# Expert weights in four buffers, and their loads queued block by block

## The chip, the cores and the metric

The kernel runs on one NeuronCore of a Trainium2 chip. The metric is the device time of one execution in microseconds; the program runs on one core, so its time is that core's. Three runs of the kernel before took 1793.85, 1797.31 and 1800.29 us, with a median of 1797.31.

## The reference

A small language-model tower of two layers works on 16 sequences of 128 tokens with rows of 192 numbers, in float32: embedding and layer norm, a Mamba block with a gated feed-forward, a mixture of experts, causal attention with 12 heads, and a second mixture of experts beside a shared gated feed-forward. The change is in the two mixtures. Both send each token to its two best experts:

```python
# layer 0: 8 experts, inner width 768;  x: the normed rows, e: an expert
y_e = relu(x @ W1[e].T + b1[e]) @ W2[e].T + b2[e]
# layer 1: 16 experts, inner width 512
y_e = (silu(x @ w1[e].T) * (x @ w3[e].T)) @ w2[e].T
# both: e, f are the router's two best of the token, g and k its weights
h = h + g * y_e + k * y_f
```

## The kernel before

Tokens are held as rows, 128 to a tile, 16 tiles. For each mixture the router gives every token a place in a DRAM array `sorted`, where each expert has a region of its own; GpSimd scatters the normed rows there (line 381). The array is then worked through in blocks of 128 rows, each of one expert: 40 blocks in the first mixture (`NB0`), 48 in the second (`NB1`). `rid` and `eid` hold the first row and the expert of each block. The results are stored in `expert`, a DRAM array of blocks, and gathered and added at the end.

All engines run the loop over blocks in pairs; block 0 of a pair uses the buffers with k = 0, the other those with k = 1. For one pair:

- SyncE (`expert_loads`, lines 301 to 327) loads the rows of both blocks (`xb`, 96 KB each, line 316), reads both expert numbers into registers, loads both first weights (`ew_in`, line 321: 576 KB in the first mixture, 768 KB in the second, over 96 partitions), then both second weights (`ew_out`, line 326: 675 KB with the biases in the first mixture, 384 KB in the second, over 128 partitions). Before each load it waits until its buffer is free. All of these go to one queue in program order.
- TensorE (`expert_blocks`) multiplies the turned rows with the first weight (24 matmul instructions a block in the first mixture, 32 in the second, line 715), turns the rows of the next pair (`turn`, line 978), and then makes the output products with the second weight (12 and 8 instructions a block).
- ScalarE applies Relu with the bias, which is part of `ew_out` (line 657, six instructions a block), or Silu in the second mixture (line 701). It waits for the second weight first in the first mixture.
- VectorE (`expert_rows_out`) copies the turned rows out of PSUM (line 1518), multiplies the two halves in the second mixture (line 1526), and adds the output bias (line 1537) or copies the output (line 1535) into `yb`, of which there are two. Before that it waits until `yb` was stored. Its drain then releases the second weight's buffer (semaphore `s_w2f`, line 1539). TensorE's drain (line 993) releases the first weight's (`s_w1f`).
- GpSimd (`store_blocks`) stores `yb` (line 468), waits for the landing and releases `yb`, one block after the other.

The buffers have two of each kind. The semaphores `s_w1`, `s_w2`, `s_w1f` and `s_w2f` exist once for each mixture and each k.

Of the kernel before, what the change touches and what calls it, by code (L numbers as in the profile page):

```python
# [9 lines left out]
ALU = mybir.AluOpType  # L10
AXX = mybir.AxisListType.X
ds = bass.ds

P = 128
B = 16
D = 192
# [41 lines left out]
def tower(nc, tok, seg, tok_tab, seg_tab, pos_tab, consts, rows, cols, w_pick, w_in, w_gate, w_x, w_dt, w_out,  # L58
          w_up, w_gf, w_down, w_r1, w_r2, w_qk, w_v, w_proj, w_g, w_s1, w_s3, w_s2, e0_in, e0_out, e1_in, e1_out,
          out):  # L60
    with ExitStack() as ctx:
# [42 lines left out]
        ew_in = [w[0:KH, :] for w in ew_in_all]  # L104
# [17 lines left out]
        def part(n, words, parts=P):  # L122
            return arena[0:parts, n:n + words]
# [28 lines left out]

        xb = [part(6144 + 256 * k, D) for k in range(2)]
# [47 lines left out]
        s_w1 = [[sem(f"s_w1_{m}{k}") for k in range(2)] for m in range(2)]  # L201
        s_w2 = [[sem(f"s_w2_{m}{k}") for k in range(2)] for m in range(2)]
        s_xb = [[sem(f"s_xb_{m}{k}") for k in range(2)] for m in range(2)]
        s_w1f = [[sem(f"s_w1f_{m}{k}") for k in range(2)] for m in range(2)]
        s_w2f = [[sem(f"s_w2f_{m}{k}") for k in range(2)] for m in range(2)]
# [80 lines left out]
        def _(sp):  # L286
# [205 lines left out]
        def _(act):  # L492
# [159 lines left out]
            with act.Fori(0, NB0 // 2) as i:  # L652
                for k in range(2):
                    act.wait_ge(s_w2[0][k], i * 16 + 16)
                    act.wait_ge(s_bh[0], i * 2 + k + 1)
                    for f in range(EF0):
                        act.activation(hbT[k][:, f, :], ps[:, 1 + 2 * k + f // 4, (f % 4) * P:(f % 4 + 1) * P], ACT.Relu,  # L657
                                       bias=ew_out[k][:, EF0 * D + f:EF0 * D + f + 1])
                    act.drain().then_inc(s_ba[0], 1)
# [46 lines left out]
        def _(pe):  # L706
# [259 lines left out]
            def expert_blocks(m, nb, fg, gated):  # L966
                for k in range(2):
                    pe.sem_inc(s_xbf[m][k], 1)
                    pe.sem_inc(s_w1f[m][k], 1)
                    pe.sem_inc(s_w2f[m][k], 1)  # L970
                n_in = fg * P

                def turn(i):

                    for k in range(2):
                        pe.wait_ge(s_xb[m][k], i * 16 + 16)
# [4 lines left out]
                def pair(i, more):  # L981
                    for k in range(2):
                        pe.wait_ge(s_bx[m], i * 2 + k + 1)
                        pe.wait_ge(s_w1[m][k], i * 16 + 16)
                        for half in range(2 if gated else 1):
                            for f in range(fg):
                                bank = 1 + 2 * k + (half if gated else f // 4)
                                base = 2 * n_in * half
                                last = accumulate(ps[:, bank, (f % 4) * P:(f % 4 + 1) * P],
                                                  [(ew_in[k][:, base + c * n_in + f * P:base + c * n_in + (f + 1) * P], xbT[k][:, c, :])  # L990
                                                   for c in range(2)])
                        last.then_inc(s_bh[m], 1)
                        pe.drain().then_inc(s_w1f[m][k], 1)
                    if more:
                        turn(i + 1)
# [151 lines left out]
        def _(ve):  # L1147
# [363 lines left out]
            def expert_rows_out(m, nb, gated):  # L1511
# [3 lines left out]
                def turn(i):  # L1515
                    for k in range(2):
                        ve.wait_ge(s_bt[m], i * 2 + k + 1)
# [4 lines left out]
                def pair(i, more):  # L1522
                    if gated:
                        for k in range(2):
                            ve.wait_ge(s_bg, i * 2 + k + 1)
# [3 lines left out]
                    if more:  # L1529
                        turn(i + 1)  # L1530
                    for k in range(2):
                        ve.wait_ge(s_by[m], i * 2 + k + 1)
                        ve.wait_ge(s_ybf[m][k], i + 1)
                        if gated:
                            last = ve.tensor_copy(yb[k], ps[:, 5 + k, 0:D])  # L1535
                        else:
                            last = ve.tensor_tensor(yb[k], ps[:, 5 + k, 0:D], ew_out[k][:, EF0 * D + EF0:], ALU.add)
                        last.then_inc(s_yb[m], 1)
                        ve.drain().then_inc(s_w2f[m][k], 1)

                turn(0)
                with ve.Fori(0, nb // 2 - 1) as i:
                    pair(i, True)
                pair(nb // 2 - 1, False)
# [212 lines left out]
```

## Time and profile before

| | |
|---|---|
| median of three runs | 1797.31 us |
| the profiled execution | 1797.96 us, its span 1796.3 us |
| mean granted TensorE clock | 0.847 of full speed |
| TensorE matmul busy | 1335.5 us (74%) |
| VectorE / ScalarE / GpSimd busy | 819.6 / 496.1 / 495.2 us |
| DMA, mean over the span | 85 GB/s, 152.92 MB |
| first expert stage | from 698 to 972 us |
| second expert stage | from 1441 to 1742 us |

The profile is of one execution. Busy time is what an engine spends in instructions that compute; times in the rows are microseconds from the start of the span. An idle stretch is put down to what ended it: `<-DMA ew_in<-in_e_in` is the landing of that transfer, `<-issue` nothing that the profile shows. `POOL` is GpSimd, `DVE` VectorE, `ACT` ScalarE, `PE` TensorE, `PEld` its weight loads and `SPq` SyncE's sequencer, which issues the loads.

### The profile page before, as it was taken

How to read it: one execution, taken by the hardware profiler on the slowest of the kernel's cores; microseconds unless marked ns; L12 is line 12 of the kernel's file. 1: busy time of each engine (PE TensorE's matmuls, PEld its weight loads, DVE VectorE, ACT ScalarE, POOL GpSimd, SP SyncE). 2: the span in 40 equal slices, each digit the busy share in tenths (PEclk: the TensorE clock that was granted, in tenths of full speed). 3: DMA queues.
4: the chain of work that ended last, by engine and by line, in shares of the span. 5: the costliest groups of instructions: out<-in, count | busy, mean ns of one | idle time of the engine just before them, and what ended most of it. 6: DMA issues, size and time to landing. Idle time of an engine off the chain costs nothing.

```text
span 1796.3 us, 23568 instructions
## 1 busy us (share of the span) xinstructions
PE 1335.5 (74%) x7336; PEld 911.8 (51%) x7336; DVE 819.6 (46%) x1551; ACT 496.1 (28%) x834; POOL 495.2 (28%) x394
## 2 busy tenths in 40 slices
PE   0656787777778673877884678989988878999960
PEld 0211232332333263877774464756657468888850
DVE  2488975865888752111111735355453312222212
ACT  0435455446435201222221213315150100101000
POOL 4655743544544441000002400000001500000025
PEclk9868787888889785999997668897988889999985
DMA  5200000000000016777774100000000267888853
GB/s 117 40 1 1 0 1 0 1 1 1 1 1 1 12 43 191 236 211 224 229 226 131 50 0 1 1 0 0 0 1 12 97 167 219 240 233 241 239 145 94
DMA packets 56059, 152.92 MB, mean 85 GB/s; under 512 B 9632, under 2 KB 30880, under 8 KB 51200
## 3 DMA queue, kind: packets, MB, share of 16 engines
q1 hardware_dynamic: 44096, 127.80, 25.1%
q0 software_dynamic: 11904, 24.40, 4.7%
q8 instruction: 30, 0.49, 0.1%
q14 instruction: 29, 0.24, 0.0%
HBM read 133.09 MB, written 19.07 MB: 85 GB/s over the span
## 4 chain that ended last, share of the span: by engine, by line
PE 34%; DMA 23%; DVE 15%; issue 11%; POOL 5%; ACT 3%; POOLq 3%; DVEq 3%; SPq 1%; ACTq 1%; PEldq 0%
PE ps L715 23%; DMA expert<-arena 21%; DVE arena L1417 4%; PE ps L843 3%; PE ps L1075 2%; POOL arena L480 2%; DVE ps L1412 2%; PE ps L868 1%; DMA ew_in<-in_e_in 1%; ACT arena L583 1%; PE ps L1067 1%; DVE st L1173 1%; POOL h_rows L346 1%; ACT arena L677 1%; PE ps L710 1%
## 5 line engine op out<-in xcount | busy, mean ns | idle before, releaser
L715 PE MATMUL ps<-arena,ew_in 96*128 96x128 f32 x2496 | 308.5, 283 | 41.3 <-DMA ew_in<-in_e_in 25.0
L715 PEld LDWEIGHTS ps<-arena,ew_in 96*128 96x128 f32 x2496 | 294.4, 196 | 58.5 <-DMA ew_in<-in_e_in 34.0
L1417 DVE TENSOR_TENSOR_SCAN arena<-arena,ps 128x1024 f32<-128x1024 f32 x96 | 219.5, 2287 | 13.4
L715 PE MATMUL ps<-xTF,wreg 96*128 96x512 f32 x352 | 204.0, 726 | 9.5 <-DVE arena L1573 4.6
L843 PE MATMUL ps<-arena,pick 32*128 32x512 f32 x384 | 133.9, 781 | 94.9 <-DVE arena L1417 91.9
L468 POOL DMA_DIRECT2D expert<-arena x88 | 47.9, 544 | 543.1 <-DVE arena L1535 190.7
L381 POOL DMA_INDIRECT sorted<-x_rows,row_i x64 | 63.5, 992 | 416.8 <-DVEq L1322 398.1
L583 ACT ACTIVATE arena<-ps,wreg 128x508 f32<-128x508 f32 x192 | 121.0, 681 | 203.9 <-PE ps L855 203.1
L715 PE MATMUL ps<-xT,wreg 96*128 96x512 f32 (+3 forms) x296 | 134.8, 602 | 29.1 <-ACT arena L544 15.6
L715 PE MATMUL ps<-ew_out,arena 128*128 128x192 f32 x864 | 152.7, 333 | 1.0 <-issue 0.5
L715 PEld LDWEIGHTS ps<-ew_out,arena 128*128 128x128 f32 x864 | 144.1, 195 | 1.6 <-issue 0.8
L855 PE MATMUL ps<-arena,pick 32*128 32x512 f32 x384 | 135.4, 785 | 8.1 <-POOLq L389 7.3
L715 PEld LDWEIGHTS ps<-xTF,wreg 96*128 96x128 f32 x352 | 75.4, 228 | 107.8 <-issue 90.1
L843 PEld LDWEIGHTS ps<-arena,pick 32*128 32x128 f32 x384 | 35.9, 221 | 173.9 <-issue 166.5
L657 ACT ACTIVATE arena<-ps,ew_out 128x128 f32<-128x128 f32 x240 | 66.4, 376 | 206.2 <-DMA ew_out<-in_e_out 158.0
L1412 DVE TENSOR_TENSOR ps<-ps,arena 128x1024 f32<-128x1024 f32 x96 | 117.1, 1220 | 9.5 <-PE ps L843 4.1
L1526 DVE TENSOR_TENSOR arena<-arena,ps 128x512 f32<-128x512 f32 x48 | 33.0, 688 | 180.0 <-ACTq L702 179.5
L715 PEld LDWEIGHTS ps<-xT,wreg 96*128 96x128 f32 (+1 forms) x296 | 58.6, 209 | 102.9 <-issue 59.9
L701 ACT ACTIVATE arena<-ps 128x512 f32<-128x512 f32 x48 | 28.7, 598 | 279.7 <-PE ps L715 279.7
L408 POOL TENSOR_TENSOR ew_out<-arena 128x1024 f32<-128x1024 f32 x32 | 75.9, 2372 | 99.8 <-DVE arena L1417 98.1
L1518 DVE COPY arena<-ps 96x256 f32<-96x256 f32 x88 | 37.0, 421 | 143.3 <-PE ps L978 130.8
L408 POOL TENSOR_TENSOR ew_in<-arena 128x1024 f32<-128x1024 f32 x32 | 76.6, 2394 | 90.1 <-DVE arena L1417 89.3
(199 smaller groups left out, 1699.6 us busy)
## 6 DMA issues: line engine op xcount, KB each, us to landing
ew_in<-in_e_in SPq DMA_DIRECT2D x48, 768.0 KB, 6.1
ew_out<-in_e_out SPq DMA_DIRECT2D x40, 675.0 KB, 4.3
ew_in<-in_e_in SPq DMA_DIRECT2D x40, 576.0 KB, 5.6
ew_out<-in_e_out SPq DMA_DIRECT2D x48, 384.0 KB, 4.0
arena<-sorted SPq DMA_DIRECT2D x88, 96.0 KB, 2.6
expert<-arena POOLq DMA_DIRECT2D x88, 96.0 KB, 4.2
sorted<-zero SPq DMA_DIRECT2D x26, 96.0 KB
wreg<-in_w_s SPq DMA_DIRECT2D x3, 768.0 KB, 11.3
```

The lines of the kernel that those rows point to most:

```text
L381: pool.indirect_dma_start(sorted_rows[m], bass.IndirectOffsetOnAxis(row_i[:, r, t:t + 1], 0), x_rows[:, t, :], None).then_inc(s_scat[m], 16)
L408: pool.tensor_tensor(hc[k % 6].rearrange("p (x t) -> p x t", x=2), hid[k % 3].rearrange("p (x t) -> p x t", x=2), Ct[c % 2].rearrange("p ( ...
L468: pool.dma_start(expert_rows[m][ds((i * 2 + k) * P, P), :], yb[k]).then_inc(s_yo[m][k], 16)
L480: pool.indirect_dma_start(g[:, t, :], None, expert_rows[m], bass.IndirectOffsetOnAxis(pos_i[:, r, t:t + 1], 0)).then_inc(s_g[m], 16)
L583: act.activation(o[:, :, 1:P], t[:, :, 1:P], ACT.Exp, scale=neg_a[:, j:j + 1]).then_inc(s_dec, 1)
L657: act.activation(hbT[k][:, f, :], ps[:, 1 + 2 * k + f // 4, (f % 4) * P:(f % 4 + 1) * P], ACT.Relu, bias=ew_out[k][:, EF0 * D + f:EF0 * D ...
L715: last = pe.matmul(o, lhs, rhs, start=(n == 0), stop=(n == len(pairs) - 1))
L843: last = pe.matmul(ps[:, U_BANK[k % 2] + x, :], pick[r, K_U + i * P:K_U + (i + 1) * P], uT[c % 2][r, g, :], start=True, stop=True)
L855: pe.matmul(ps[:, DT_BANK + x, :], pick[r, K_U + i * P:K_U + (i + 1) * P], dtT[c % 2][r, g, :], start=True, stop=True).then_inc(s_dtf, 1)
L1412: ve.tensor_tensor(bx, bx, Bt[c % 2].rearrange("p (a t) -> p a t", a=1).broadcast_to((P, 2, CN)), ALU.mult)
L1417: ve.tensor_tensor_scan(hid[k % 3], dec[k % 3], bx.rearrange("p x t -> p (x t)"), 0.0, ALU.mult, ALU.add)\
L1518: ve.tensor_copy(xbT[k], ps[0:KH, 7 * k, 0:2 * P].rearrange("p (c t) -> p c t", c=2))\
```

## The change

Each weight has four buffers. Two stay where they were; two more for each lie in a part of `arena` (from word 11264) that no one else uses in these stages. `e_in[m][j]` and `e_out[m][j]` name the four buffers of mixture m. All loops over pairs become loops over four blocks (j = 0 to 3, two pairs, h = 0 and 1), with half as many turns; `xb`, `xbT`, `hbT`, `yb` and PSUM keep two of each (k = j % 2). The four semaphores of the weights go on counting from the first mixture to the second (`QUADS`). SyncE queues rows, first weight and second weight of one block, and then those of the next. TensorE gets a wait of its own for the addition of block n-2 before it writes that PSUM bank again.

```diff
+        EW = 11264
+        e_in = [[w[0:KH, :] for w in ew_in_all] + [part(EW + step * x, n, KH) for x in range(2)]
+                for step, n in ((2886, 1536), (2816, 2048))]
+        e_out = [[w[:, :] for w in ew_out] + [part(EW + step * x + n, step - n) for x in range(2)]
+                 for step, n in ((2886, 1536), (2816, 2048))]
+        QUADS = (0, NB0 // 4)
...
-                with sp.Fori(0, nb // 2) as i:
-                    for k in range(2):
-                        sp.wait_ge(s_xbf[m][k], i + 1)
+                with sp.Fori(0, nb // 4) as i:
+                    for j in range(4):
+                        k = j % 2
+                        sp.wait_ge(s_xbf[m][k], i * 2 + j // 2 + 1)
                         sp.nop(nofuse=True)
-                        r = sp.value_load(rid[0:1, ds(i * 2 + k, 1)], min_val=0, max_val=ne * REG)
+                        r = sp.value_load(rid[0:1, ds(i * 4 + j, 1)], min_val=0, max_val=ne * REG)
                         sp.dma_start(xb[k], sorted_rows[m][ds(r, P), :]).then_inc(s_xb[m][k], 16)
-                    e = [sp.value_load(eid[0:1, ds(i * 2 + k, 1)], min_val=0, max_val=ne - 1) for k in range(2)]
-                    for k in range(2):
-                        sp.wait_ge(s_w1f[m][k], i + 1)
+                        e = sp.value_load(eid[0:1, ds(i * 4 + j, 1)], min_val=0, max_val=ne - 1)
+                        sp.wait_ge(s_w1f[j], i + QUADS[m] + 1)
                         sp.nop(nofuse=True)
-                        sp.dma_start(ew_in[k][:, 0:n_in], t_in[ds(e[k], 1), :, :].rearrange("a p n -> (a p) n"))\
-                          .then_inc(s_w1[m][k], 16)
-                    for k in range(2):
-                        sp.wait_ge(s_w2f[m][k], i + 1)
+                        sp.dma_start(e_in[m][j][:, 0:n_in], t_in[ds(e, 1), :, :].rearrange("a p n -> (a p) n"))\
+                          .then_inc(s_w1[j], 16)
+                        sp.wait_ge(s_w2f[j], i + QUADS[m] + 1)
                         sp.nop(nofuse=True)
-                        sp.dma_start(ew_out[k][:, 0:n_out], t_out[ds(e[k], 1), :, :].rearrange("a p n -> (a p) n"))\
-                          .then_inc(s_w2[m][k], 16)
+                        sp.dma_start(e_out[m][j][:, 0:n_out], t_out[ds(e, 1), :, :].rearrange("a p n -> (a p) n"))\
+                          .then_inc(s_w2[j], 16)
...
                     for k in range(2):
-                        pe.wait_ge(s_ba[m], i * 2 + k + 1)
-                        pe.wait_ge(s_w2[m][k], i * 16 + 16)
-                        accumulate(ps[:, 5 + k, 0:D], [(hbT[k][:, f, :], ew_out[k][:, f * D:(f + 1) * D]) for f in range(fg)])\
+                        j = 2 * h + k
+                        pe.wait_ge(s_ba[m], i * 4 + j + 1)
+                        pe.wait_ge(s_w2[j], i * 16 + at + 16)
+                        pe.wait_ge(s_w2f[(j + 2) % 4], i + QUADS[m] + 1 + h)
+                        accumulate(ps[:, 5 + k, 0:D], [(hbT[k][:, f, :], e_out[m][j][:, f * D:(f + 1) * D]) for f in range(fg)])\
                             .then_inc(s_by[m], 1)
 
-                turn(0)
-                with pe.Fori(0, nb // 2 - 1) as i:
-                    pair(i, True)
-                pair(nb // 2 - 1, False)
+                turn(0, 0)
+                with pe.Fori(0, nb // 4 - 1) as i:
+                    pair(i, 0, True)
+                    pair(i, 1, True)
+                pair(nb // 4 - 1, 0, True)
+                pair(nb // 4 - 1, 1, False)
```

## Rows read from the trace of the kernel before

**Rows 1.** The page: the chain that ended last, shares of the span by line.

```profile
PE ps L715 23%; DMA expert<-arena 21%; DVE arena L1417 4%; PE ps L843 3%; PE ps L1075 2%; POOL arena L480 2%; DVE ps L1412 2%; PE ps L868 1%; DMA ew_in<-in_e_in 1%; ACT arena L583 1%; PE ps L1067 1%; DVE st L1173 1%; POOL h_rows L346 1%; ACT arena L677 1%; PE ps L710 1%
```

**Rows 2.** Windows: us, busy time of each engine, granted clock, DMA share, GB/s.

```profile
721.60:955.40 233.80, 192.14 (x1370) 179.85 (x1368) 28.02 (x72) 59.80 (x216) 19.03 (x36) 0.98 0.75 226
1465.00:1726.40 261.40, 240.13 (x1852) 227.20 (x1850) 64.60 (x133) 26.32 (x44) 23.95 (x44) 0.99 0.84 232
...
1565.00:1590.00 25.00, 23.32 (x185) 22.15 (x183) 5.94 (x13) 2.99 (x5) 2.17 (x4) 1.00 0.88 252
```

**Rows 3.** Chain of 830 to 885 us, by line.

```profile
by line: DMA expert<-arena 87.0%; issue 11.9%; POOLq L471 1.7%; POOLq L468 1.2%; POOLq L464 1.0%; POOLq L466 0.3%; POOLq L470 0.2%; POOLq L467 0.2%; POOLq L469 0.2%
```

**Rows 4.** Pieces of the chain in both stages: start, us, what.

```profile
829.03 4.07 DMA expert<-arena
834.12 7.27 DMA expert<-arena
842.66 4.08 DMA expert<-arena
...
967.08 1.91 DMA expert<-arena
...
1563.91 3.88 DMA expert<-arena
1568.81 5.25 DMA expert<-arena
```

**Rows 5.** Timeline, first stage, TensorE: start, us, instructions, [idle before <- what ended it].

```profile
721.63 2.84 PE L715 MATMUL ps<-arena,ew_in 96*128 96x128 f32 x24
728.52 0.67 PE L978 MATMUL ps<-cst,arena 128*96 128x128 f32 x4 [0.77 <-DMA arena<-sorted]
732.92 2.84 PE L715 MATMUL ps<-arena,ew_in 96*128 96x128 f32 x24
...
955.46 2.92 PE L715 MATMUL ps<-arena,ew_in 96*128 96x128 f32 x24 [0.21 <-DMA ew_in<-in_e_in]
```

**Rows 6.** Timeline, second stage, TensorE.

```profile
1465.20 3.74 PE L715 MATMUL ps<-arena,ew_in 96*128 96x128 f32 x32
1476.57 3.84 PE L715 MATMUL ps<-arena,ew_in 96*128 96x128 f32 x32
1492.52 5.47 PE L715 MATMUL ps<-arena,ew_in 96*128 96x128 f32 x32 [2.89 <-DMA ew_in<-in_e_in]
...
1570.83 0.64 PE L978 MATMUL ps<-cst,arena 128*96 128x128 f32 x4 [0.26 <-issue]
...
1726.36 3.81 PE L715 MATMUL ps<-arena,ew_in 96*128 96x128 f32 x32 [0.66 <-DMA ew_in<-in_e_in]
```

**Rows 7.** Timeline, first stage, all engines, one pair.

```profile
847.17 0.95 SPq L321 DMA_DIRECT2D ew_in<-in_e_in  x2
...
847.77 0.54 POOL L468 DMA_DIRECT2D expert<-arena  x1 [4.56 <-issue]
...
854.80 0.36 DVE L1537 TENSOR_TENSOR arena<-ps,ew_out 128x192 f32<-128x192 f32 x1 [4.74 <-POOLq L471]
...
857.08 1.57 SPq L316 DMA_DIRECT2D arena<-sorted  x2
...
859.59 1.66 ACT L657 ACTIVATE arena<-ps,ew_out 128x128 f32<-128x128 f32 x6 [1.93 <-DMA ew_out<-in_e_out]
```

**Rows 8.** Waits of 640 to 1000 us: total, times, longest.

```profile
ACT arena L657 <- DMA ew_out<-in_e_out: 158.0, 33, 8.4
DVE arena L1537 <- POOLq L471: 77.5, 18, 5.4
```

**Rows 9.** Timeline, start of the first stage.

```profile
701.37 0.24 PEld L978 LDWEIGHTS ps<-cst,arena 128*96 128x96 f32 x2 [1.10 <-DMA arena<-sorted]
...
701.67 0.97 SPq L321 DMA_DIRECT2D ew_in<-in_e_in  x2
...
706.32 5.49 PE L715 MATMUL ps<-arena,ew_in 96*128 96x128 f32 x24 [4.29 <-DMA ew_in<-in_e_in]
```

More of the change, by code:

```diff
@@ L103, in tower @@
         ew_in_all = [sb(f"ew_in{k}", [P, 2048]) for k in range(2)]
-        ew_in = [w[0:KH, :] for w in ew_in_all]
         ew_out = [sb(f"ew_out{k}", [P, EF0 * D + EF0 + D]) for k in range(2)]
@@ L200, in tower @@
         s_scat = [sem(f"s_scat{m}") for m in range(2)]
-        s_w1 = [[sem(f"s_w1_{m}{k}") for k in range(2)] for m in range(2)]
-        s_w2 = [[sem(f"s_w2_{m}{k}") for k in range(2)] for m in range(2)]
+        s_w1 = [sem(f"s_w1_{k}") for k in range(4)]
+        s_w2 = [sem(f"s_w2_{k}") for k in range(4)]
         s_xb = [[sem(f"s_xb_{m}{k}") for k in range(2)] for m in range(2)]
-        s_w1f = [[sem(f"s_w1f_{m}{k}") for k in range(2)] for m in range(2)]
-        s_w2f = [[sem(f"s_w2f_{m}{k}") for k in range(2)] for m in range(2)]
+        s_w1f = [sem(f"s_w1f_{k}") for k in range(4)]
+        s_w2f = [sem(f"s_w2f_{k}") for k in range(4)]
         s_xbf = [[sem(f"s_xbf_{m}{k}") for k in range(2)] for m in range(2)]
@@ L651, in _ @@
             route_exp(0, E0)
[L652 to L655, printed above, removed]
+            with act.Fori(0, NB0 // 4) as i:
+                for j in range(4):
+                    k, w = j % 2, e_out[0][j]
+                    act.wait_ge(s_w2[j], i * 16 + 16)
+                    act.wait_ge(s_bh[0], i * 4 + j + 1)
                     for f in range(EF0):
                         act.activation(hbT[k][:, f, :], ps[:, 1 + 2 * k + f // 4, (f % 4) * P:(f % 4 + 1) * P], ACT.Relu,
-                                       bias=ew_out[k][:, EF0 * D + f:EF0 * D + f + 1])
+                                       bias=w[:, EF0 * D + f:EF0 * D + f + 1])
                     act.drain().then_inc(s_ba[0], 1)
@@ L968, in expert_blocks, with turn @@
                     pe.sem_inc(s_xbf[m][k], 1)
-                    pe.sem_inc(s_w1f[m][k], 1)
-                    pe.sem_inc(s_w2f[m][k], 1)
+                if m == 0:
+                    for j in range(4):
+                        pe.sem_inc(s_w1f[j], 1)
+                        pe.sem_inc(s_w2f[j], 1)
                 n_in = fg * P
-                def turn(i):
+                at = QUADS[m] * 16
+                def turn(i, h):
                     for k in range(2):
-                        pe.wait_ge(s_xb[m][k], i * 16 + 16)
+                        pe.wait_ge(s_xb[m][k], i * 32 + h * 16 + 16)
                         for c in range(2):
@@ L979, in turn, with pair @@
                         last.then_inc(s_bt[m], 1)
-                def pair(i, more):
+                def pair(i, h, more):
                     for k in range(2):
-                        pe.wait_ge(s_bx[m], i * 2 + k + 1)
-                        pe.wait_ge(s_w1[m][k], i * 16 + 16)
+                        j = 2 * h + k
+                        pe.wait_ge(s_bx[m], i * 4 + j + 1)
+                        pe.wait_ge(s_w1[j], i * 16 + at + 16)
                         for half in range(2 if gated else 1):
@@ L1513, in expert_rows_out, with turn @@
                     ve.sem_inc(s_ybf[m][k], 1)
-                def turn(i):
+                def turn(i, h):
                     for k in range(2):
-                        ve.wait_ge(s_bt[m], i * 2 + k + 1)
+                        ve.wait_ge(s_bt[m], i * 4 + 2 * h + k + 1)
                         ve.tensor_copy(xbT[k], ps[0:KH, 7 * k, 0:2 * P].rearrange("p (c t) -> p c t", c=2))\
@@ L1520, in turn, with pair @@
                         ve.drain().then_inc(s_xbf[m][k], 1)
-                def pair(i, more):
+                def pair(i, h, more):
                     if gated:
                         for k in range(2):
-                            ve.wait_ge(s_bg, i * 2 + k + 1)
+                            ve.wait_ge(s_bg, i * 4 + 2 * h + k + 1)
                             ve.tensor_tensor(hbT[k][:, 0:EF1, :], hbT[k][:, 0:EF1, :],
@@ L1528, in pair @@
                             ve.drain().then_inc(s_ba[m], 1)
-                    if more:
-                        turn(i + 1)
+                    if h == 0:
+                        turn(i, 1)
+                    elif more:
+                        turn(i + 1, 0)
                     for k in range(2):
-                        ve.wait_ge(s_by[m], i * 2 + k + 1)
-                        ve.wait_ge(s_ybf[m][k], i + 1)
+                        j = 2 * h + k
+                        ve.wait_ge(s_by[m], i * 4 + j + 1)
+                        ve.wait_ge(s_ybf[m][k], i * 2 + h + 1)
                         if gated:
@@ L1536, in pair @@
                         else:
-                            last = ve.tensor_tensor(yb[k], ps[:, 5 + k, 0:D], ew_out[k][:, EF0 * D + EF0:], ALU.add)
+                            last = ve.tensor_tensor(yb[k], ps[:, 5 + k, 0:D], e_out[0][j][:, EF0 * D + EF0:EF0 * D + EF0 + D], ALU.add)
                         last.then_inc(s_yb[m], 1)
[L1539 to L1544, printed above, removed]
+                        ve.drain().then_inc(s_w2f[j], 1)
+                turn(0, 0)
+                with ve.Fori(0, nb // 4 - 1) as i:
+                    pair(i, 0, True)
+                    pair(i, 1, True)
+                pair(nb // 4 - 1, 0, True)
+                pair(nb // 4 - 1, 1, False)
             expert_rows_out(0, NB0, False)
```

11 lines of the change are left out of this document (7 added, 4 removed).

## The prediction

> **What bounds the kernel now.** I read four views in order: busy time and the chain of the whole program, the same for the two expert stages, the durations of the transfers in that chain, then one pair of blocks instruction by instruction.
>
> The chain gives 21% of the span to one transfer, the store of a block's output rows to DRAM (`expert<-arena`, line 468), nearly as much as to all of TensorE's work under line 715 [rows 1]. TensorE is busy 82% of 233.8 us in the first expert stage and 92% of 261.4 us in the second, while the DMA engines are busy 75% and 84% [rows 2]: neither is full in the first. In 55 us of the first stage the store alone is 87% of the chain [rows 3].
>
> GpSimd does the stores one at a time: wait for the rows, issue, wait for the landing, release the row buffer. From issue to landing a store takes 1.91 us at the end of the stage, when nothing else is being moved; in the middle, the first of a pair takes 4.08 and the second 7.27 us [rows 4]. From a landing to the next issue pass 1.02 us (834.12 less 829.03 and its 4.07) and 1.27 us (842.66 less 834.12 and its 7.27), together 2.29. So the loop of two stores is 4.08 + 7.27 + 2.29 = 13.6 us. From the second pair to the last, the first stage takes (955.46 - 721.63) / 18 = 12.99 us a pair [rows 5]. The store loop is the clock of that stage.
>
> It is closed through the change's own wait. VectorE's addition of the second block waits for the row buffer, and so for the earlier store (77.5 us, 18 times) [rows 8]; only then does SyncE queue that block's second weight, and ScalarE, which reads the bias in it, waits (158.0 us, 33 times). In one pair: two first-weight loads are issued at 847.17, the store at 847.77, the addition follows at 854.80, the rows of the next pair are issued at 857.08 (behind the late second weight in SyncE's program), ScalarE gets its bias at 859.59 [rows 7]. The second store is slow because it is issued just behind two 576 KB loads.
>
> What TensorE alone would take: 732.92 - 721.63 = 11.29 us for a pair, with a wait of 0.77 us for rows in it that is 0.26 where nothing is late [rows 5, 6]: 10.78 us. In the second stage an undisturbed pair is 1476.57 - 1465.20 = 11.37 us and the mean (1726.36 - 1465.20) / 22 = 11.87 [rows 6]. There the loop of the stores is 3.88 + 5.25 + 2.29 = 11.4 us [rows 4], equal to TensorE's pair; no activation reads the second weight.
>
> **The change part by part.**
>
> 1. Four buffers of each weight. The second weight of block n is queued when block n-4 is added up, one whole pair earlier. ScalarE's waits for the bias and TensorE's for first weights go. This is worth nothing by itself beyond TensorE's own 10.78 us: what is late next is the store loop, or the DMA engines.
>
> 2. The order on SyncE: rows, first, second weight of one block, then the next block. Two first-weight loads no longer go out within 1 us; a second weight and its wait lie between. The store of a pair's first block now probably stands behind a first and a second weight, that of the second behind one load or a part of it. Bounds for two landings: 2 x 1.91 = 3.8 us (nothing ahead) and 4.08 + 7.27 = 11.35 us (as now); the loop is then 6.1 to 13.6 us. The nearest row is the second stage, where the two first weights are spread by a wait: 3.88 + 5.25 for loads of 768 KB, a loop of 11.4. A 576 KB load is three quarters of that, so the part of 5.25 above 1.91 shrinks from 3.34 to 2.5 us: 3.88 + 4.42 + 2.29 = 10.6 us. The deeper queue speaks for somewhat more. I take 11.3 us for the first stage, TensorE at 10.78 with clock dips (granted clock 0.98, nearly always its upper level of 2.4 GHz [rows 2]; 2% more, 11.0) and some store waits: 18 x (12.99 - 11.3) = 30.4 us gained. The most is 18 x (12.99 - 10.78) = 39.8.
>
> On this the Trainium skill, "DMA: Bandwidth & Descriptors" (Queues, rings and completion order), has two statements: an engine goes round-robin between queues packet by packet, and a semaphore's write lands only after every earlier write of that DMA engine, across queues. By the first alone the stores would slip in between the loads and take little over 1.91 us; the trace has 7.27, which agrees with the second. By the first the stage would come down to TensorE's pair and the time to about 1754 (39.8 and 5.9 gained, 2 lost).
>
> 3. The second stage. Its slack over 22 undisturbed pairs is 261.2 - 22 x 11.37 = 11.0 us; 4.6 of it is one pair of 15.95 us at 1476.57, whose end waits 2.89 us for a first weight after the first stores had been slow [rows 6]. With four buffers about half of the 11.0 goes: 11.6 us a pair, 5.9 us gained. Bounds: 11.0 gained; lost, 22 x (12.8 - 11.87) = 20.5 us, if both stores land in 5.25.
>
> 4. The start of each stage. TensorE turns the rows of both blocks before it multiplies. The second rows are now queued behind a first and a second weight. Now the second rows are there at 701.37, the first weight at 706.32, 4.65 us after its issue [rows 9]. Rows that follow 1.25 MB of weights, at the 252 GB/s of the fullest window [rows 2], land some 5 us after the first weight's issue, and 1.1 us of transposing and copying follow; the weight itself is issued about 1 us earlier. I take 1 us lost in each stage, 0 to 3 as bounds: 2 us. TensorE needs the second block's weight only 3 us later.
>
> 5. TensorE's new wait before the output product (the addition of block n-2 must be done) was implied by the load of the second weight until now. Behind it stand the output products and all of the next pair. It is the store loop again and costs nothing while the loop is shorter than TensorE's pair.
>
> 6. SyncE's own work. Two row loads with their register loads take 1.57 us, and a block's instructions together some 3.4, so 7 us a pair against 10.8. It is hidden; uncovered it would give 7 us, no bound. The row load of block n+1 now stands behind the wait for the second-weight buffer of block n. It is needed most of a pair later, so nothing waits. The doubled loop bodies of TensorE, VectorE and ScalarE cost no instruction on the chip's path that was not there; no row shows a longer body's fetch. Bounds 0 to 0.5 us a pass over 10 and 12 passes, 0 to 11 us; I take 0, since between the looped and the written-out last pair of now TensorE idles 0.2 us (955.46, for a weight) [rows 5].
>
> Sum: 1797.96 (span 1796.3 and 1.7 around it) - 30.4 - 5.9 + 2 = 1763.7, say 1764. The median of the runs, 1797.31, is 0.65 below the profiled one; I leave that out. What this kernel's measurement can tell from no change is about 0.3%, 5 us.
>
> **The rivals.**
>
> A. The DMA engines bound the first stage. A pair moves 2 x (576 + 675 + 96 + 96) KB = 2.955 MB. The fullest window has 252 GB/s at a share of 0.88 [rows 2]: at that rate 11.7 us a pair, at a share of 1.0 (286 GB/s) 10.3. At 11.7: 23.2 us gained there, nothing in the second stage, 2 lost: 1777. For it: the share would be 0.88 to 0.92, and 96-partition loads take most of it. Against: idle stretches between transfers vanish when they are queued.
>
> B. The store loop stays as it is, since stores stand behind two loads as before and the buffers only lengthen the queue in front of them: 12.99 and 11.87 a pair, 2 us for the start: 1797 to 1800. For it: the loop doesn't contain a weight buffer at all, only landings. Against: its 7.27 comes from two back-to-back first weights, which the new order parts.
>
> C. Slower. With two blocks more in flight, each store finds a full queue: the first of a pair lands as the second does now, 7.27, and the second as in the second stage, 5.25. First stage 14.8 us a pair, +32.6; second stage two times 5.25, 12.8 us, +20.5; start 2: about 1853. It decides as soon as two landings pass 10.7 us in the first stage or 9.6 in the second. Against: no landing of that length can last when the DMA engines idle a quarter of the time; a milder form (13.3 and 12.2) gives 1813.
>
> D. Everything hidden: 10.78 and 11.37 with 2 us for the start: 1797.96 - 39.8 - 11.0 + 2 = 1749.
>
> **How the numbers follow.** Forecast (1756 to 1770) 52%; A 17% (1770 to 1782); D 12% (1745 to 1756); B 10%; C 9%. The predicted time is the forecast's, 1764. Range 1747 to 1790: it takes in the forecast, A and D; above it lie B and C, 19%, where the working of step 2 has no case between 1782 and 1797. Faster by over 0.3%: 52 + 17 + 12 and a tenth of B, which may gain a little, 83%; within 0.3% 8%; slower 9%.
>
> **What would show it.** Step 2: pair starts of the first stage 10.8 to 11.7 us apart; landings of the two stores adding up to less than 9.2; ScalarE's wait for `ew_out` gone; SyncE's wait for line 1539's release still there but without followers. Step 3: 11.4 to 11.7 us in the second stage, DMA share above 0.84. Step 4: the first product of a stage 0 to 3 us later against its first row load. A would show as TensorE waiting for `ew_in` with the DMA share near 0.9; B and C as the store at 80% of the stage's chain with landings of 7 us. I am wrong in the main if the additions still wait 4 us for the stores in each pair.

## The result, and the profile after

Over four runs each the kernel after takes 1750.42 us in the median (1741.02 to 1757.98), the kernel before 1795.58 (1785.63 to 1800.29): a ratio of 0.9727 [0.968, 0.9774], so some 49 us less (the medians differ by 45). Here and below the ratios are of fast runs alone, while a median of times takes in a slower execution where there was one (one of four in e1 and in e2). The forecast was 1764 in a range of 1747 to 1790, so the time lies at the low edge, on the number of rival D. The profiled execution took 1757.27 us (span 1755.6), 40.7 less than the profiled one of before.

The chain of the whole program, by line (answers to [rows 1]; the matmul line 715 is now 720, the store's 468 is 472):

```profile
PE ps L720 35%; DMA expert<-arena 8%; DVE arena L1432 5%; PE ps L848 3%; PE ps L1090 3%; POOL arena L484 2%; DMA arena<-sorted 2%; DVE ps L1427 2%; PE ps L873 1%; PE ps L1082 1%; PE ps L986 1%; DVEq L1428 1%; ACT arena L587 1%; DVE st L1188 1%; POOL h_rows L350 1%
```

The store fell from 21% to 8% of the span in this chain. The windows of the two expert stages, from the second pair's start to the last's (columns as in [rows 2]):

```profile
722.70:932.50 209.80, 188.59 (x1371) 179.24 (x1370) 27.67 (x71) 59.75 (x216) 18.61 (x35) 0.98 0.84 250
1437.30:1685.80 248.50, 235.01 (x1851) 225.84 (x1850) 64.55 (x132) 26.29 (x44) 23.95 (x44) 1.00 0.88 244
```

TensorE is busy 90% and 95% of them (82% and 92% before), at 250 and 244 GB/s (226 and 232). Its pairs, by the start of the first block's hidden products (answers to [rows 5, 6]):

```profile
722.75 2.84 PE L720 MATMUL ps<-arena 96*128 96x128 f32 x24
...
733.61 2.84 PE L720 MATMUL ps<-arena,ew_in 96*128 96x128 f32 x24
...
744.35 2.84 PE L720 MATMUL ps<-arena 96*128 96x128 f32 x24
```

```profile
932.48 2.84 PE L720 MATMUL ps<-arena 96*128 96x128 f32 x24
```

```profile
1437.34 3.74 PE L720 MATMUL ps<-arena 96*128 96x128 f32 x32
...
1448.67 3.74 PE L720 MATMUL ps<-arena,ew_in 96*128 96x128 f32 x32
```

```profile
1685.76 3.74 PE L720 MATMUL ps<-arena 96*128 96x128 f32 x32
```

The first stage now takes (932.48 - 722.75) / 18 = 11.65 us a pair, where it took 12.99; an undisturbed pair is 744.35 - 733.61 = 10.74. The second takes (1685.76 - 1437.34) / 22 = 11.29, where it took 11.87. Where the 40.7 us went, between the same events of the two profiled executions:

| | before | after | difference |
|---|---|---|---|
| first stage, first row load to gather | 275.08 | 253.59 | -21.5 |
| of it, pairs 2 to 19 | 18 x 12.99 | 18 x 11.65 | -24.1 |
| of it, first row load to first product | 8.21 | 9.28 | +1.1 |
| of it, first pair | 15.3 | 17.9 | +2.6 |
| of it, last pair's start to gather | 17.73 | 16.68 | -1.05 |
| second stage, the same | 302.25 | 287.75 | -14.5 |
| of it, pairs 2 to 23 | 22 x 11.87 | 22 x 11.29 | -12.7 |
| all else, code that wasn't touched | | | -4.7 |

What still bounds the first stage is the store. The chain of 716 to 930 us by line, then its pieces from four pairs (answers to [rows 3, 4]; start, us, what):

```profile
by line: DMA expert<-arena 62.7%; PE ps L720 17.5%; issue 10.1%; DMA arena<-sorted 2.7%; DVE arena L1555 2.6%; PE ps L986 1.8%; POOLq L475 1.5%; POOLq L468 0.9%; POOLq L472 0.5%; SPq L321 0.2%; POOLq L474 0.2%; SPq L330 0.2%; POOLq L473 0.1
```

```profile
822.12 4.18 DMA expert<-arena
...
827.33 6.15 DMA expert<-arena
...
834.75 4.21 DMA expert<-arena
...
839.98 5.68 DMA expert<-arena
...
846.92 4.10 DMA expert<-arena
...
852.04 5.41 DMA expert<-arena
...
858.71 4.14 DMA expert<-arena
...
863.87 5.07 DMA expert<-arena
```

63% of the chain is landings of stores (87% in the window shown of before). The issues follow the landings by 1.03 and 1.27 us as before; 4.18 + 6.15, 4.21 + 5.68, 4.10 + 5.41 and 4.14 + 5.07 give loops of 12.6, 12.2, 11.8 and 11.5 us. From the first store of the second pair, issued at 740.22 us, to that of the eighteenth at 928.01 are 16 loops of 11.7 us on average, and TensorE's pairs take 11.65: that is the pace of the stage. Waits of 640 to 975 us, then of 1440 to 1700 (total, times, longest; the addition is line 1555, the copy of the second mixture 1553):

```profile
ACT arena L662 <- PE ps L720: 184.7, 40, 21.1
DVE arena L1555 <- POOLq L475: 150.4, 34, 6.9
```

```profile
DVE arena L1553 <- POOLq L475: 34.0, 22, 2.9
```

ScalarE's wait for `ew_out`, 158 us before [rows 8], is gone: it now waits for TensorE. VectorE's wait for the store has gone from 77.5 us in 18 waits to 150.4 in 34: in both blocks of a pair the store is now what comes last. That is 4.4 us a wait, so the sign by which the prediction was to be wrong in the main (additions that still wait 4 us for the stores in each pair) is there.

What TensorE itself waits for, beside the 0.3 us or so of "issue" at each step, in the window of the pairs of the first stage, before and then after:

```profile
PE ps L978 <- DMA arena<-sorted: 26.3, 19, 2.1
PE ps L715 <- DMA ew_in<-in_e_in: 8.7, 12, 1.3
```

```profile
PE ps L986 <- DMA arena<-sorted: 10.4, 10, 3.2
```

The wait for rows is shorter than before and the one for first weights is gone; none was or is for ScalarE. All idle time of TensorE in the window went from 41.7 to 21.2 us and its busy time from 192.1 to 188.6: so 20.5 of the 24.1 us gained are idle time.

The longest wait for rows that is left, on the timeline of all engines (`SPq` L322 loads rows, L326 a first weight, L330 a second weight):

```profile
824.31 0.33 SPq L326 DMA_DIRECT2D arena<-in_e_in  x1
...
827.15 0.33 SPq L330 DMA_DIRECT2D arena<-in_e_out  x1
...
828.38 0.33 SPq L322 DMA_DIRECT2D arena<-sorted  x1
...
833.78 0.36 DVE L1555 TENSOR_TENSOR arena<-ps,arena 128x192 f32<-128x192 f32 x1 [6.89 <-POOLq L475]
...
834.39 0.33 SPq L330 DMA_DIRECT2D arena<-in_e_out  x1
...
835.41 0.42 PE L986 MATMUL ps<-cst,arena 128*96 128x128 f32 x2 [3.23 <-DMA arena<-sorted]
...
835.67 5.78 PE L720 MATMUL ps<-ew_out,arena 128*128 128x192 f32 x24
```

```profile
837.00:841.30 4.30, 4.30 (x19) 4.30 (x19) 0.36 (x1) 0.00 (x0) 0.54 (x1) 0.64 0.99 281
```

The rows issued at 828.38 stand behind weights issued at 824.31 and 827.15, and are there for TensorE at 835.4, 7 us later. TensorE idles 3.23 us. The granted clock of the window that follows is 0.64 in the mean, so part of it at 1.2 GHz and part at 2.4, and 24 output products take 5.78 us where they otherwise take 4.07: the pair lasts 15.9 us.

The start of the first stage (answers to [rows 9]):

```profile
695.57 0.36 SPq L322 DMA_DIRECT2D arena<-sorted  x1
...
699.20 0.34 SPq L322 DMA_DIRECT2D arena<-sorted  x1
...
704.39 0.66 PE L986 MATMUL ps<-cst,arena 128*96 128x128 f32 x2 [6.20 <-DMA arena<-sorted]
...
704.85 5.33 PE L720 MATMUL ps<-arena,ew_in 96*128 96x128 f32 x24
```

The second rows leave SyncE 3.6 us after the first, behind two weights, and TensorE waits for them.

### The profile page after: what moved, and what is told of

The parts are those of the page before. It is cut to its first block, busy times and chain, and to the rows that moved or that the text cites. A ratio compares the mean times of both kernels' runs of the same rounds, so it can differ in the third digit from the quotient of the medians.

```text
span 1755.6 us, 23414 instructions
## 1 busy us (share of the span) xinstructions
PE 1325.4 (75%) x7336; PEld 911.9 (52%) x7336; DVE 819.8 (47%) x1551; ACT 495.5 (28%) x834; POOL 494.0 (28%) x394
## 4 chain that ended last, share of the span: by engine, by line
PE 48%; DVE 16%; DMA 12%; issue 9%; POOL 5%; ACT 3%; DVEq 3%; POOLq 2%; SPq 1%; ACTq 1%; PEldq 0%
PE ps L720 35%; DMA expert<-arena 8%; DVE arena L1432 5%; PE ps L848 3%; PE ps L1090 3%; POOL arena L484 2%; DMA arena<-sorted 2%; DVE ps L1427 2%; PE ps L873 1%; PE ps L1082 1%; PE ps L986 1%; DVEq L1428 1%; ACT arena L587 1%; DVE st L1188 1%; POOL h_rows L350 1%
## 5 line engine op out<-in xcount | busy, mean ns | idle before, releaser
L720 PE MATMUL ps<-arena 96*128 96x128 f32 (+1 forms) x1680 | 224.1, 290 | 8.3 <-issue 8.3
L720 PEld LDWEIGHTS ps<-arena 96*128 96x128 f32 (+1 forms) x1680 | 215.2, 192 | 12.4 <-issue 12.1
L720 PE MATMUL ps<-arena,ew_in 96*128 96x128 f32 x1248 | 154.6, 284 | 7.7 <-issue 7.7
L720 PE MATMUL ps<-xT,wreg 96*128 96x512 f32 (+3 forms) x296 | 133.9, 599 | 29.7 <-ACT arena L548 15.6
L720 PEld LDWEIGHTS ps<-arena,ew_in 96*128 96x128 f32 x1248 | 150.2, 199 | 11.5 <-issue 11.4
L412 POOL TENSOR_TENSOR arena<-arena 128x1024 f32<-128x1024 f32 x32 | 75.2, 2352 | 56.8 <-DVE arena L1432 52.8
L720 PEld LDWEIGHTS ps<-wreg,arena 128*128 128x128 f32 x480 | 82.8, 200 | 14.3 <-issue 9.4
```

The source lines that it names most:

```text
L412: pool.tensor_tensor(hc[k % 6].rearrange("p (x t) -> p x t", x=2), hid[k % 3].rearrange("p (x t) -> p x t", x=2), Ct[c % 2].rearrange("p ( ...
L720: last = pe.matmul(o, lhs, rhs, start=(n == 0), stop=(n == len(pairs) - 1))
```

## The experiments

Two theories run through them. S: the clock of the first stage is GpSimd's loop of two stores, one after the other, and what else is late hangs on it. A: the rate of the DMA engines is (rival A). In the short diffs `rows`, `w1` and `w2` are SyncE's three loads of a block with their waits. Times a pair are from the second pair to the last, first and second stage. Before: 12.99 and 11.87; after: 11.65 and 11.29. Each is read from one profiled execution. In the expectations theory D is A, and B is that the earlier loads alone bring the gain.

**The buffers alone** (`e1_four_old_order`): the kernel after, SyncE's order as before.

```diff
-  for j in range(4): rows(j); w1(j); w2(j)
+  for h in range(2): rows(2h); rows(2h+1); w1(2h); w1(2h+1); w2(2h); w2(2h+1)
```

> Four buffers, but SyncE queues as before: both rows, both first weights, both second weights. Theory S (the loop of GpSimd's two serial stores is the clock of the first stage, and the order of the loads sets how long a store takes to land): two first weights stand in front of the second store again, its landing goes from 5.7 back to some 7 us, and the first stage takes 12.3 to 13.3 us a pair instead of 11.65; the time is 1762 to 1780 where the changed kernel has 1750 (ratio to the kernel before 0.98 to 0.99). Theory B (the earlier loads alone bring the gain, the order is nothing): within 3 us of the changed kernel, ratio 0.973, first stage 11.65 a pair. Theory D (the DMA engines' rate bounds the first stage): as B, since the same bytes move.

1784.25 us, ratio 0.984 [0.9767, 0.9913]; 12.60 and 11.51 a pair. After the first pair the first stage runs five at 10.73 to 10.78 us and then goes over to pairs of 11.0 to 15.7 for good; in the second stage 19 of 22 take 11.22 to 11.27, and two 13.5 and 15.2. TensorE's wait is the new one of the change, for the addition, and so for the store:

```profile
PE ps L724 <- DVEq L1561: 22.2, 11, 3.5
```

So buffers without the order bring 1.6% by the ratios, and the order the other 1.1% of 0.9727. That split isn't sharp: the two intervals touch, and e1's executions spread from 1766.63 to 1797.73, its profiled one (1790.55) near the top. The paces, 12.60 against 11.65, point the same way.

**Blocks in turn, with two buffers** (`e2_two_alternating`): the kernel before; rows of both blocks, then first and second weight of one, first and second of the other.

```diff
-  w1(0); w1(1); w2(0); w2(1)
+  w1(0); w2(0); w1(1); w2(1)
```

> The kernel before with two buffers; only the order on SyncE is changed: both rows, then first weight, second weight of block 0, first weight, second weight of block 1. Theory S: the second store of a pair stands behind less, but the second weight still comes late, so ScalarE waits for its bias: 12.0 to 12.8 us a pair in the first stage instead of 12.99, second stage 11.5 to 12.2, time 1780 to 1797 (ratio 0.99 to 1.0). Theory B: no gain at all, ratio 1.0 or above, since the first weight of block 1 now waits for a second-weight buffer.

2047.63 us, ratio 1.1328 [1.1253, 1.1403]; 17.77 and 18.72 a pair. Missed. SyncE and TensorE in one pair:

```profile
840.31 0.33 SPq L321 DMA_DIRECT2D ew_in<-in_e_in  x1
...
851.40 0.34 SPq L325 DMA_DIRECT2D ew_out<-in_e_out  x1
...
852.66 0.34 SPq L321 DMA_DIRECT2D ew_in<-in_e_in  x1
...
860.27 2.05 PE L714 MATMUL ps<-arena,ew_in 96*128 96x128 f32 x8 [5.01 <-DMA ew_in<-in_e_in]
```

The second block's first weight (852.66) stands behind the first block's second weight (851.40), which waits for a buffer that is free late; TensorE then waits 5.01 us for the first weight. What stands in front of a load in the queue counted, and not its own buffer alone. The order of the change needs the four buffers.

**Two stores in flight** (`e3_stores_overlap`): the kernel after; GpSimd issues the next block's store before it waits for the landing of the last.

```diff
+  store(0)
   for each block n:
-      store(n); wait for its landing; nop; drain -> yb free
+      store(n+1); wait for the landing of n; nop; drain -> yb free
```

> The changed kernel, but GpSimd issues the next block's store before it waits for the landing of the one before (two in flight, still two row buffers). Theory S: the store loop no longer adds up both landings; the first stage falls from 11.65 to TensorE's own 10.8 to 11.1 us a pair, 10 to 15 us less than the changed kernel: ratio to the kernel before 0.964 to 0.968, time 1732 to 1741. The second stage stays at 11.25 to 11.35. Theory D: the first stage stays at 11.65 (253 GB/s), time as the changed kernel, within 3 us, and TensorE now waits for first weights or rows.

1771.8 us, ratio 0.9832 [0.9777, 0.9886]; 11.77 and 11.98 a pair: nothing gained in the first stage and the second slower. Both theories missed. The chain of 880 to 935 us shows why (line 471 is the store, 474 the wait for a landing, 476 the drain):

```profile
by line: POOLq L476 72.2%; issue 9.4%; DMA arena<-sorted 7.9%; PE ps L728 7.7%; DVE arena L1563 5.3%; POOL expert L471 3.4%; POOLq L471 1.1%; SPq L321 0.9%; PE ps L994 0.8%; SPq L330 0.7%; POOLq L474 0.3%; POOLq L470 0.2%; DVEq L1559 0.2%; 
...
886.66 0.54 POOL expert L471
887.20 5.50 POOLq L476
...
893.90 0.06 POOL expert L471
894.00 4.04 POOLq L476
```

The drain behind the issue at 886.66 lasts 5.50 us, to 892.70, and this store lands 5.96 us after its issue, at 892.6. The wait for the earlier landing has 0.3% of the chain: that landing had come. The new theory, G: GpSimd's drain ends only when its outstanding stores have landed, so the stores were never two.

**The same without a drain** (`e5_overlap_no_drain`):

```diff
-      nop; drain -> yb free
+      sem_inc -> yb free
```

> As the run with overlapping stores (two in flight, two row buffers), but GpSimd releases a row buffer by a plain semaphore increment behind its wait, not by a drain. Theory G (a drain on GpSimd also waits for the landing of the store that was issued just before it, so the stores were never two in flight): now they are; the first stage goes from 11.77 to 10.8 to 11.2 us a pair, the time to a ratio of 0.963 to 0.970 to the kernel before. Theory W (it is the landing's own length, 5 to 7 us behind loads, times two buffers): no change against that run, 11.7 a pair, ratio 0.980 to 0.985.

1741.65 us, ratio 0.9693 [0.9654, 0.9731]; 10.77 and 11.30 a pair. GpSimd's timeline has the stores 1.9 us apart:

```profile
808.32 0.54 POOL L471 DMA_DIRECT2D expert<-arena  x1 [8.35 <-DVE arena L1562]
810.18 0.54 POOL L471 DMA_DIRECT2D expert<-arena  x1 [1.32 <-DVE arena L1562]
```

A `sem_inc` in place of the nop and the drain is all that differs from e3, and it makes the difference between 11.77 and 10.77: the drain is shown, and so is S, since the stage now runs at TensorE's own pair, and the additions wait for no store. The landings are not shorter (median 5.6 us; 4.4 after).

**Four buffers for output rows** (`e4_four_row_buffers`): the kernel after with drains, `yb` four deep, two stores issued ahead.

```diff
-  yb = [part(8704 + 256 * k, D) for k in range(2)]
+  yb = [part(n, D) for n in (8704, 8960, 17152, 17408)]
```

> The changed kernel with four buffers for the output rows as well and up to three stores in flight. Theory S: the first stage at 10.8 to 11.0 us a pair; time 0 to 4 us below the run with two overlapping stores, ratio 0.962 to 0.967. Theory D: as the changed kernel, 11.65 a pair.

1739.81 us, ratio 0.9662 [0.9614, 0.971]; 10.80 and 11.39. The window of the first stage's pairs, and the chain of 716 to 916 us (matmuls are line 732, transposes 998):

```profile
722.90:916.70 193.80, 182.65 (x1367) 175.64 (x1366) 28.01 (x72) 59.58 (x216) 18.98 (x36) 1.00 0.89 272
```

```profile
by line: PE ps L732 77.3%; DMA arena<-sorted 10.5%; issue 6.1%; PE ps L998 5.6%; SPq L321 1.0%; SPq L323 0.6%; SPq L322 0.5%; DVE arena L1546 0.4%; SPq L330 0.4%; SPq L326 0.4%; DVEq L1548 0.1%; SPq L320 0.0%; SPq L325 0.0%; SPq L329 0.0%; 
```

The DMA engines move 272 GB/s at a share of 0.89, more than the 250 of after, and the chain holds neither a weight nor a store: TensorE has 83% of it, the landings of rows 10.5%. A is refuted for the pace of after.

**Two stores in flight on the kernel before** (`e6_before_overlap`): the edit of e5 with two weight buffers and the old order.

> The kernel before (two weight buffers, old order) with its two row buffers, and the stores two in flight by a semaphore increment in place of the drain. Theory S (the serial stores were the clock of its first stage): 11.2 to 12.2 us a pair instead of 12.99 there, second stage 11.3 to 11.6 instead of 11.87, ratio 0.976 to 0.988, so more than half of the change's gain without a single further weight buffer. Rival (the late second weight is a clock of its own at two buffers): 12.6 to 13.0 a pair, ratio 0.995 to 1.0.

1767.99 us, ratio 0.9833 [0.9803, 0.9864]; 11.50 and 11.57. ScalarE still waits for the bias:

```profile
ACT arena L664 <- DMA ew_out<-in_e_out: 151.7, 35, 8.2
```

So 1.49 us a pair can be had with no buffer of the change at all. It isn't ScalarE's wait that holds TensorE, though: TensorE's own waits, 16.6 us in 18, are for rows, which SyncE queues behind the late second weight. The four buffers with the same old order (e9, below) end them and bring 11.50 and 11.57 to 10.73 and 11.23: the other 0.77 and 0.34 us a pair.

**Four buffers for output rows, old order** (`e7_four_rows_old_order`): e4 with SyncE's order of e1.

> Four row buffers and four weight buffers, but SyncE queues both rows, both first weights, both second weights. Theory S: with the loop of the stores loosened by four row buffers the order matters only through the sum of two landings: if it stays under TensorE's pair, 10.8 a pair as with the new order, ratio 0.963 to 0.969; the older order has 4.1 + 7.3 us of landing, a loop of some 13 us with serial stores, and then the first stage is at 12 to 13 us a pair again, ratio 0.978 to 0.985. I expect the second.

1754.06 us, ratio 0.9733 [0.9694, 0.9771]; 11.74 and 11.46. Between the two expectations: eight pairs in a row at 10.73 to 10.80 us, then 10.8 to 15.1. With drains the order is still worth 0.94 us a pair.

**Stores in flight, old order** (`e9_overlap_old_order`): e5 with SyncE's order of e1.

> Four weight buffers, stores two in flight without the drain, but SyncE queues both rows, both first weights, both second weights. Theory S (the order counts only by what stands in front of serial stores): 10.75 to 11.0 us a pair in the first stage, as with the new order (10.77), ratio 0.966 to 0.972. Rival O (two first weights back to back are too late or too long by themselves): 11.5 to 12.5 a pair, ratio 0.974 to 0.982.

1741.18 us, ratio 0.9716 [0.9693, 0.974]; 10.73 and 11.23, as e5 or a little below. Once no store waits for another, the order is worth nothing. It had worked through the landings alone.

**Fewer bytes** (`e8_second_weight_once`): the kernel after with the loop of stores as it is. In the first mixture the second weight is loaded once, that of expert 0, into all four buffers, and per block only the biases; the output of the first mixture is therefore another.

```diff
-  each block: e_out[j] <- second weight and biases, 675 KB
+  once: e_out[j] <- second weight of expert 0;  each block: e_out[j] <- biases
```

> The changed kernel, but in the first stage the second weights of expert 0 are loaded once into the four buffers, and each block then loads only its biases (99 KB instead of 675 KB): the second product uses a wrong expert's weight, and 47% fewer bytes move there. Theory S: a store stands behind less, its landings fall from 4.2 + 5.7 to under 4 + 4, and TensorE's pair is the clock: 10.75 to 10.85 us a pair instead of 11.65, first stage 15 us shorter, 3 us lost to the four loads ahead; second stage unchanged. Time 10 to 15 us under the changed kernel, ratio 0.964 to 0.968. Rival (a landing's length has nothing to do with the loads): 11.65 a pair, ratio 0.973 to 0.976.

1756.15 us, ratio 0.976 [0.9727, 0.9794]; 10.73 and 11.43. The pace is S's, the total not: the four loads ahead of the stage put its first product at 720.4 us (704.9 after), 15.6 us later, where I had counted 3. (The bytes of the stage are 40% fewer, not 47%.) The window of the pairs:

```profile
735.00:930.00 195.00, 184.14 (x1383) 177.73 (x1382) 28.02 (x72) 60.40 (x220) 19.99 (x37) 1.00 0.58 162
```

At 162 GB/s the landings take 1.9 to 2.5 us and 4.1 to 4.8 in turn, with few exceptions (median 2.4), so the loop of two comes to 8.9 us or so, and TensorE runs free with the serial stores. The landing's length is set by the loads about it.

**Weights ahead of the scatter** (`e10_weights_ahead`, `e11_four_rows_ahead`): e5, and e5 with the four `yb` of e4, where the weights of the first four blocks are queued before SyncE waits for the scattered rows.

```diff
-  wait for the scatter; each block: rows, w1, w2
+  w1(0), w2(0) ... w1(3), w2(3); wait for the scatter; rows of blocks 0 to 3; then as before
```

> The run with two stores in flight and no drain (first stage 10.77 us a pair, ratio 0.969), and the first four blocks' weights are queued before SyncE waits for the scattered rows; then four row loads, then the loop. If the start is bound by the landing of a weight and of rows behind it: from a stage's first row load to its first product 2.5 to 4 us instead of 9.3, 5 to 6 us less in each stage, ratio 0.960 to 0.966. Rival: 5 MB of weights ahead slow the scatters of the rows, which run at that time on the same DMA engines, and give the gain back: first row load 3 to 6 us later, ratio 0.967 to 0.970.

> Four row buffers, three stores in flight, no drain, and the weights ahead as in the run beside it. The stores have slack in both, so within 3 us of it, ratio 0.959 to 0.966; if the second stage's small waits (11.30 a pair against 11.24) come from row buffers, 1 to 2 us less.

1761.55 us, ratio 0.9828 [0.9802, 0.9854], and 1755.78 us, 0.9799 [0.9772, 0.9825]: both 14 to 20 us slower by the medians than without it (e5, e9, e12). TensorE and SyncE at the start of e10's first stage:

```profile
701.99 0.37 SPq L326 DMA_DIRECT2D ew_in<-in_e_in  x1
...
709.29 17.55 SPq L319 DMA_DIRECT2D arena<-sorted  x3
...
724.55 1.09 PE L1007 MATMUL ps<-cst,arena 128*96 128x128 f32 x4 [36.72 <-DMA arena<-sorted]
725.81 1.43 PE L741 MATMUL ps<-arena,ew_in 96*128 96x128 f32 x5 [0.17 <-DVE arena L1554]
```

The rows are issued at 709.29 into a queue of four blocks' weights, 4 x 1251 KB, some 20 us at the 250 GB/s of the stage. The first product is at 725.8 us, and at 716.4 in e11, where after had 704.9. The row load itself leaves 6 us later than in e5, counted from SyncE's first zeroing store (19.9 against 13.8 us), as the rival had it: SyncE is busy issuing eight weights from 701.99 on. GpSimd issues its scatters in as long a time as in e5 (10.1 us), so that they were slowed isn't shown. The hope failed: the rows were what was missing, not the weights.

**Four row buffers, no drain** (`e12_four_rows_no_drain`): e4 with `sem_inc` for the drain.

> Four weight buffers, four row buffers, up to three stores in flight, the row buffer released by a semaphore increment, rows and weights queued block by block. TensorE is the clock of both stages already with two row buffers (10.77 and 11.30 a pair) and with four and the drain (10.80 and 11.39), so nothing is left for the stores to give: 10.75 to 10.8 and 11.25 to 11.35 a pair, ratio 0.966 to 0.972, the same as those two within the interval. If row buffers still cost something in the second stage, 11.24 there and 1 to 2 us less.

1739.92 us, ratio 0.9693 [0.9663, 0.9722]; 10.80 and 11.31. No better than e4 or e5: either decouples the stores. These are the quickest versions, some 10 us below the kernel after by the medians; their intervals overlap its own, so the totals alone don't show it, while the paces do.

## Why the prediction was wrong, and where it held

**The steps that failed.** The time is in the range, but the sum doesn't hold term by term, and it comes close only because errors cancel. Step 1 put the buffers by themselves at nothing: in e1 they give 0.39 and 0.36 us a pair with the order unchanged, 7 and 8 us over the stages. Step 3 put the second stage at 5.9 us: it gave 12.7, more than twice that. Step 2 had the two landings too short, 3.88 + 4.42, and so the loop of the stores under TensorE's pair, at 10.6 us: it takes 11.7, still above. Step 6 said of the rows "nothing waits": TensorE waits 10.4 us for them.

**What bounds before, and step 2.** The store loop was the clock: e5 changes nothing but the stores' overlap against after and gives TensorE's pair, e6 does it on the kernel before and takes 1.49 us of each pair. The mechanism of step 2 also held: against e1 the order takes the first stage from 12.60 to 11.65 with the loop unchanged, and it has no effect where the loop is open (e9). Its size was too large: 30.4 us forecast for the first stage, 24.1 measured, of which the order has 17.1 and the buffers 7.0. The landings add up to 9.2 to 10.3 in the four pairs shown, and to 9.4 over the stage (the loop of 11.7 less 2.3). The sign "less than 9.2" was just missed, the pace of 11.65 is near the top of "10.8 to 11.7", and the sign of being wrong in the main, additions that wait 4 us for the stores in each pair, came true: they wait 4.4 us, 34 times. In e4 and e5, where the stores are off the path, they wait for no store.

On the skill's two rules: a store lands in 1.91 us with nothing about it [rows 4], 2.4 in the median with e8's 162 GB/s and 4.4 with the 250 of after. The Trainium skill, "DMA: Bandwidth & Descriptors" (Queues, rings and completion order), lets a semaphore's write land after every earlier write of that engine; the traces agree. By its round-robin alone the stores would have come down to little over 1.91 with the change, and they did not. No run tells the waiting for earlier writes from a plain sharing of the DMA engines' rate.

**Step 1** said that the buffers are worth nothing by themselves beyond TensorE's own pair, which is the store loop's to give. Beside what they give in e1, they give 0.77 and 0.34 us a pair on top of open stores (e9 against e6, both with the old order). I had looked at ScalarE's wait for the bias, but no wait of TensorE's is for ScalarE, before or in e6; it waits for rows that are queued behind the late second weight. Whether the bias would be next, had the rows come in time, no run shows.

**Step 3** was mis-sized the most: 5.9 us forecast, 12.7 measured. I halved a slack of 11.0 us, and the 11.37 that I took for an undisturbed pair still had lateness in it: after has 11.22 to 11.24 in 11 of its 22. Against 11.23 the slack was 14 us, and nearly all of it went; e1's 0.36 us a pair make 8 of it the buffers' own.

From the forecast, 1763.7, to the profiled 1757.27 there are 6.4 us. Step 3 gave 6.8 more than its term, step 2 6.3 less; the starts cost 0.4 and not 2 (1.6 more), the first pairs of the two stages cost 1.6 (2.6 less 0.9), their ends gave 1.2, and the untouched code gave 4.7: together 6.4. That steps 2 and 3 nearly cancel is luck. One of the chances is off as well: 52, 17, 12 and a tenth of B's 10 make 82% for "faster", not 83.

**Step 4.** The first product of the first stage came 1.1 us later against its row load, as forecast, and for the reason given; that of the second 0.7 us earlier. What I left out is the first pair, 2.6 us longer at a lower clock (24 hidden products of the second block took 5.46 us, 4.79 before).

**Step 6** said of rows behind the wait for a second-weight buffer "nothing waits". Wrong, and it was wrong of the kernel before too, where TensorE waits 26.3 us for rows. They stand behind two weights in the queue as well, and TensorE still waits 10.4 us for them, 10 times, with a clock dip behind the longest. Of the 18 x (11.65 - 10.74) = 16.4 us that the first stage has left that is the larger part; most of the rest is busy time, 188.6 us at a mean granted clock of 0.98 against 182.7 at 1.00 for the same work in e5. Since e5 with the same order has 10.77, those waits hang on the stores too: the second weight in front is queued only after an addition, and the addition waits for a store.

**Step 5** held: in the window of the pairs TensorE has no wait for the addition, though the loop is longer than its pair. With the old order it has 22.2 us of it (e1), so the cover was thin.

**The rivals.** A: refuted by e4, which moves 272 GB/s with no weight and no store in the chain. B and C: the landings became shorter, not longer. D named the right time for the median, but not the mechanism: the first stage is not hidden (11.65, not 10.78), the second is better than D had it (11.29, not 11.37), and 4.7 us lie in code that wasn't touched. What these 4.7 us are stays open. They are of the size of the spread between runs of one kernel (1741 to 1758), and the first stage's first row load is anywhere from 695.6 to 703.9 us in kernels that are the same up to there. The median is 7 us below the profiled run as well; so the time by the median owes as much to that as to the terms of the sum.

## What to carry to other kernels

Look for the loop whose every step waits for a landing, and count what is queued in front of it. Deeper buffers elsewhere left this one in place (a loop of 11.7 us), while a second store in flight took it off the path. Check that the release of the buffer isn't itself a wait for the newest transfer. A load that the next step needs soon (here 96 KB of rows) must not be queued behind large ones that nobody needs yet.

## What the hardware showed that I had not expected

- GpSimd's drain waited for its own outstanding store: 5.50 and 4.04 us, from just after the issue to within 0.1 us of the landing, in e3; with `sem_inc` in its place stores were issued 1.86 us apart (e5).
- The pace has two regimes in one execution: e1 ran 5 pairs and e7 8 at 10.73 to 10.81 us and then fell to 11 to 15.7 (e7 has one more of 10.84).
- An idle stretch of TensorE of 3.23 us was followed by a granted clock of 0.64 over 4.3 us; it cost 1.7 us beyond the idle time.
